# Expert tiles of the second layer in split precision, and second weights that stay resident in the third layer

## The reference

```
# L1: layernorm with gain and shift, 8 experts, top 2, capacity = ceil(2 * 1792 / 8) = 448 tokens each
hmid    = gelu(einsum('ecd,edf->ecf', exp_in, W1) + b1)     # 256 -> 1024
exp_out = einsum('ecf,efd->ecd', hmid, W2) + b2             # 1024 -> 256
x       = x + sum over the 2 chosen experts of exp_out * gate
# L2: layernorm, 8 experts, top 1, no capacity
h = relu(einsum('nd,edm->enm', x, W1) + b1)                 # 256 -> 1024
y = einsum('enm,emd->end', h, W2) + b2                      # 1024 -> 256
x = x + y[chosen expert] * probability
```

## Time and profile before

| | us |
|---|---|
| median of 3 runs | 3487.58 (3485.43 to 3488.54) |
| the profiled execution | 3493.5, of which the span of its instructions is 3491.7 |
| tile stage L0t | about 519.6 to 790.3 |
| tile stage L1t | about 1252.0 to 1483.4 |
| tile stage L2t | about 2266.2 to 2445.3 |

### The profile page before, as it was taken

The page is one execution under the profiler, slowest core; times in us unless marked ns, Lnnn a source line. Parts: engine busy times, 40 slices in busy tenths (PEclk is TensorE's granted clock), DMA queues, the critical chain, the costliest instruction groups (busy, mean ns, idle before and its releaser), DMA issues. The chain is left out here.

```text
span 3491.7 us, 60671 instructions
## 1 busy us (share of the span) xinstructions
PE 3171.1 (91%) x21982; PEld 2617.9 (75%) x21982; DVE 1555.4 (45%) x3343; ACT 1527.9 (44%) x4145; POOL 1308.9 (37%) x1417
## 2 busy tenths in 40 slices
PE   5888869998989869989999999699899999996999
PEld 4777758996666646668888887588788888875998
DVE  4777750004566520044444444300444444445766
ACT  2555524443355512245555555234455555552332
POOL 0000001113100011057777776310577777773343
PEclk8999959999999879999999999699999999997999
DMA  6556536542100234110000000298000000001433
GB/s 145 131 133 137 118 130 204 182 166 82 38 1 1 88 93 119 60 32 15 15 15 15 15 13 1 77 320 276 27 13 13 13 13 13 11 1 44 120 103 90
DMA packets 154741, 269.25 MB, mean 77 GB/s; under 512 B 50396, under 2 KB 129753, under 8 KB 140393
## 3 DMA queue, kind: packets, MB, share of 16 engines
q1 hardware_dynamic: 140840, 239.95, 23.2%
q0 software_dynamic: 8064, 20.20, 2.2%
q10 hardware_dynamic: 5568, 5.51, 0.5%
HBM read 231.13 MB, written 34.46 MB: 76 GB/s over the span
## 5 line engine op out<-in xcount | busy, mean ns | idle before, releaser
L718 POOL TENSOR_SCALAR L_probs<-L_probs,L_inverse 112x375 f32<-112x375 f32 x512 | 653.0, 1275 | 119.5 <-issue 119.5
L866 DVE TENSOR_REDUCE L_negmax<-bank 112x1 f32<-112x375 f32 x768 | 394.6, 542 | 431.7 <-PE bank L470 356.9
L674 ACT ACTIVATE L_probs<-bank,L_negmax 112x375 f32<-112x375 f32 x768 | 435.2, 572 | 219.6 <-DVE L_negmax L866 214.7
L497 PE MATMUL bank<-ident,L_probs 112*125 112x112 f32 x2304 | 399.6, 282 | 21.2 <-POOL L_probs L718 15.4
L497 PEld LDWEIGHTS bank<-ident,L_probs 112*125 112x125 f32 x2304 | 338.8, 190 | 92.6 <-issue 50.9
L716 POOL TENSOR_TENSOR L_inverse<-L_sums,neg_one 112x1 f32<-112x1 f32 x512 | 297.1, 580 | 142.2 <-ACT L_probs L674 141.8
L654 ACT ACTIVATE L_probsT<-bank 125x336 f32<-125x336 f32 x512 | 231.9, 453 | 248.1 <-PE bank L497 248.1
L636 ACT ACTIVATE v<-bank 125x512 f32<-125x512 f32 x192 | 114.8, 598 | 267.4 <-PE bank L423 267.4
L704 POOL TENSOR_TENSOR L_stats<-L_stats,neg_half 112x1 f32<-112x1 f32 x48 | 27.1, 564 | 517.7 <-DVE L_stats L783 517.7
L512 PE MATMUL bank<-L_probsT,v 125*64 125x112 f32 x3072 | 206.1, 269 | 2.4 <-ACT L_probsT L654 1.1
L416 PE MATMUL bank<-L_ctx_hi,L_wk_hi 128*128 128x376 f32 x512 | 149.3, 373 | 29.8 <-DVE L_ctx_lo L850 22.1
(11 more groups left out here) (305 smaller groups left out, 6968.0 us busy)
## 6 DMA issues: line engine op xcount, KB each, us to landing
L2t_w<-in_F_w SPq DMA_DIRECT2D x42, 1024.0 KB, 5.1
L0t_w<-in_F_w SPq DMA_DIRECT2D x35, 1024.0 KB, 5.0
L_keys<-spread_k SPq DMA_DIRECT2D x64, 376.0 KB, 6.4
L_ctxT<-in_ctxT SPq DMA_DIRECT2D x48, 375.0 KB, 3.3
tile_w<-in_F_w SPq DMA_DIRECT2D x16, 1024.0 KB, 5.8
L3d_row<-comb_rows SPq DMA_DIRECT2D x64, 224.0 KB, 3.3
w_all<-in_F_w SPq DMA_DIRECT2D x8, 1024.0 KB, 13.6
L_q<-spread_q SPq DMA_DIRECT2D x128, 56.0 KB, 2.2
```

The source lines that it names most:

```text
L497: ins = pe.transpose(psT[h % len(psT)][0:SJ, j * T:(j + 1) * T], probs[h % NB][:, j * SJ:(j + 1) * SJ], core.ident[0:T, 0:T])
L674: act.activation(probs[e % NB][:, :], psS[e % 2][0:T, 0:S], ACT.Exp, bias=negmax[b.par][:, e:e + 1], accum_out=sums[b.par][:, e:e + 1]).th ...
L718: pool.tensor_scalar(probs[h % NB][:, :], probs[h % NB][:, :], inverse[b.par][:, h:h + 1], None, ALU.mult)\
L866: dve.tensor_reduce(negmax[b.par][:, h:h + 1], psS[h % 2][0:T, 0:S], AX, ALU.max, negate=True).then_inc(maxed.sem, 1)
```

## The change

L1's tile stage is a new function, `capacity_tiles`. A tile is still one expert with 448 tokens. ScalarE rounds `w1`, `w2` to their hi halves (copies of 128x2048); VectorE makes their lo halves, both halves of the gathered rows and both halves of each hidden part of 128x448. TensorE runs three fp32r products for each float32 product before. The `w2` product is turned: the weights are now stationary and 448 tokens stream, so its output is transposed (`yT`); VectorE adds `b2`, TensorE transposes it back (8 transposes, `turn_out`), and ScalarE takes it out. The weights have one raw buffer each and are split a tile ahead; `b1`, `b2`, gain and shift of all experts are loaded in the routing stage.

L2's tile stage becomes `resident_tiles`, which L0 uses already: `w2` of all 8 experts is loaded in the routing stage, and the 4 MB for the cross attention of L3 move from the routing stage to tile 1 of the tile stage.

```diff
@@ -1499,6 +1499,8 @@
                 load(1)
                 for t in range(NT):
                     if t == 1:
+                        sp.wait_ge(all_weights.sem, all_weights.at(16 * E))
                         for dst, src, sem in next_loads:
                             sp.dma_start(dst, src).then_inc(sem, 16)
                     if t + 2 < NT:
...
+def capacity_tiles(nc, core, name, w, tile, NT, func):
+...
+                for e in range(NT):
+                    if e + 1 < NT:
+                        (w1_to, w1_from, w1_sem), (w2_to, w2_from, w2_sem) = cap_weights(core, w, e + 1)
+                        sp.wait_ge(w1_split.sem, w1_split.at(e + 1))
+                        sp.dma_start(w1_to, w1_from).then_inc(w1_sem, 16)
+                        sp.wait_ge(w2_split.sem, w2_split.at(e + 1))
+                        sp.dma_start(w2_to, w2_from).then_inc(w2_sem, 16)
+                    if e:
+                        store(e - 1)
+                store(NT - 1)
+...
+                def gather(e):
+                    if e >= 2:
+                        pool.wait_ge(xT_made.sem, xT_made.at(e - 1))
+                    for c in range(CH):
+                        pool.indirect_dma_start(
+                            out=xs[e % 2][:, c, :], out_offset=None, in_=core.tokens[:, :],
+                            in_offset=bass.IndirectOffsetOnAxis(ap=core.rows_of[0:CW, e * CH + c:e * CH + c + 1], axis=0))\
+                            .then_inc(rows_here[e % 2].sem, 16)
+...
+                def up(e, f):
+                    if f == 0:
+                        pe.wait_ge(w1_split.sem, w1_split.at(e + 1))
+                        pe.wait_ge(x_split.sem, x_split.at(e + 1))
+                    pe.wait_ge(h_taken.sem, h_taken.at(F * e + f - 1))
+                    for m, (wt, x) in enumerate(((w1_hi, x_hi), (w1_hi, x_lo), (w1_lo, x_hi))):
+                        for k in range(DC):
+                            ins = pe.matmul(psH[f % 2][:, 0:tile], wt[:, k, f * P:(f + 1) * P], x[:, k, :],
+                                            start=(m + k == 0), stop=(m + k == DC + 1))
+                    ins.then_inc(h_made.sem, 1)
+                def down(e, f):
+                    if f == 0:
+                        pe.wait_ge(w2_split.sem, w2_split.at(e + 1))
+                        pe.wait_ge(y_taken.sem, y_taken.at(e))
+                    pe.wait_ge(low.sem, low.at(F * e + f + 1))
+                    for half in range(DC):
+                        at = slice(half * P, (half + 1) * P)
+                        for m, (wt, h) in enumerate(((w2_hi[e % 2], h_hi), (w2_hi[e % 2], h_lo), (w2_lo[e % 2], h_hi))):
+                            ins = pe.matmul(psY[half][:, 0:tile], wt[:, f, at], h[:, f, :],
+                                            start=(f + m == 0), stop=(f == F - 1 and m == 2))
+                    if f == F - 1:
+                        ins.then_inc(y_made.sem, 1)
+                def turn_out(e):
+                    pe.wait_ge(y_taken.sem, y_taken.at(e + 1))
+                    for i in range(2):
+                        pe.wait_ge(y_out.sem, y_out.at(2 * e + i - 1))
+                        for c in range(2):
+                            at = (2 * i + c) * CW
+                            for half in range(DC):
+                                ins = pe.transpose(psO[i][0:CW, c * D + half * P:c * D + (half + 1) * P],
+                                                   yT[:, half, at:at + CW], core.ident[:, :])
+                        ins.then_inc(y_turned.sem, 1)
+                turn_in(0)
+                for e in range(NT):
+                    for f in range(F):
+                        up(e, f)
+                        if e and f == 2:
+                            turn_out(e - 1)
+                    if e + 1 < NT:
+                        turn_in(e + 1)
+                    for f in range(F):
+                        down(e, f)
+                turn_out(NT - 1)
+...
+                def high_w1(e):
+                    act.wait_ge(w1_here.sem, w1_here.at(16 * e + 16))
+                    act.wait_ge(h_made.sem, h_made.at(F * e))
+                    act.activation(w1_hi[:, :, :], w1[:, :, :], ACT.Copy).then_inc(w1_high.sem, 1)
+...
+                def hidden_part(e, f):
+                    n = F * e + f
+                    act.wait_ge(h_made.sem, h_made.at(n + 1))
+                    act.wait_ge(low.sem, low.at(n - 1))
+                    act.activation(hidden[n % 2][:, :], psH[f % 2][:, 0:tile], func, bias=b1[:, e, f:f + 1])\
+                        .then_inc(h_taken.sem, 1)
+                act.wait_ge(small.sem, small.at(64))
+                high_w1(0)
+                take_xT(0)
+                high_w2(0)
+                for e in range(NT):
+                    for f in range(F):
+                        hidden_part(e, f)
+                        if e and f == 4:
+                            take_out(e - 1)
+                    if e + 1 < NT:
+                        high_w1(e + 1)
+                        take_xT(e + 1)
+                        high_w2(e + 1)
+                take_out(NT - 1)
+...
+                def split_x(e):
+                    dve.wait_ge(xT_taken.sem, xT_taken.at(e + 1))
+                    dve.wait_ge(h_made.sem, h_made.at(F * e))
+                    dve.tensor_copy(x_hi[:, :, :], xT[:, :, :])
+                    dve.drain()
+                    dve.tensor_tensor(x_lo[:, :, :], xT[:, :, :], x_hi[:, :, :].bitcast(F32), ALU.subtract)\
+                        .then_inc(x_split.sem, 1)
+...
+                def split_hidden(e, f):
+                    n = F * e + f
+                    dve.wait_ge(h_taken.sem, h_taken.at(n + 1))
+                    if f == 0:
+                        dve.wait_ge(y_made.sem, y_made.at(e))
+                    dve.tensor_copy(h_hi[:, f, :], hidden[n % 2][:, :])
+                    dve.drain()
+                    dve.tensor_tensor(h_lo[:, f, :], hidden[n % 2][:, :], h_hi[:, f, :].bitcast(F32), ALU.subtract)\
+                        .then_inc(low.sem, 1)
+                def take_y(e):
+                    dve.wait_ge(y_made.sem, y_made.at(e + 1))
+                    dve.wait_ge(y_turned.sem, y_turned.at(2 * e))
+                    for half in range(DC):
+                        ins = dve.tensor_scalar(yT[:, half, :], psY[half][:, 0:tile], b2[:, e, half:half + 1], None, ALU.add)
+                    ins.then_inc(y_taken.sem, 1)
+                dve.wait_ge(small.sem, small.at(64))
+                split_w1(0)
+                split_x(0)
+                split_w2(0)
+                for e in range(NT):
+                    for f in range(F):
+                        split_hidden(e, f)
+                    if e + 1 < NT:
+                        split_w1(e + 1)
+                        split_x(e + 1)
+                        split_w2(e + 1)
+                    take_y(e)
...
     def tile_loads(w):
         out = []
-        for e in range(2):
-            for n in ("w1", "b1", "w2", "b2"):
-                src = w[n][e].partition_broadcast(T) if n == "b2" else w[n][e]
-                dst = h[f"tile_{n}_{e}"]
-                out.append((dst[everything[len(dst.shape)]], src, sem(f"w_here{e}")))
-        return out
+        for n in CAP_HELD[2:]:
+            out.append((h["cap_" + n][everything[len(h["cap_" + n].shape)]], w[n], sem("small_here")))
+        return cap_weights(core, w, 0) + out
...
-                    lambda: expert_tiles(nc, core, "L1t", f1, CAPACITY, TILES["L1"], ACT.Gelu, False))),
+                    lambda: capacity_tiles(nc, core, "L1t", f1, CAPACITY, TILES["L1"], ACT.Gelu))),
             lambda: cross_attention(nc, core, "L2", a["ctxT"], l2, 64, topk=2)),
         lambda: held(
             wide,
-            routing("L2", f2, 1, "all", TILE, lambda: wide_loads(l3)),
-            lambda: expert_tiles(nc, core, "L2t", f2, TILE, TILES["L2"], ACT.Relu, True),
+            lambda: held({"w2_all": [P, 8, 8, D]},
+                         routing("L2", f2, 1, "all", TILE, lambda: resident_loads(f2)),
+                         lambda: resident_tiles(nc, core, "L2t", f2, TILE, TILES["L2"], ACT.Relu, wide_loads(l3))),
```

111 lines of the change are left out of this document (106 added, 5 removed).

## The result

| | before | changed |
|---|---|---|
| median of 4 runs, us | 3488.06 (3485.43 to 3490.5) | 3450.32 (3441.31 to 3457.09) |
| ratio to before (95% interval) | | 0.9876 [0.9853, 0.9898] |
| span of the profiled execution, us | 3491.7 | 3448.0 |

The change makes the kernel 1.24% faster, 37.7 us by the medians. Forecast were 3443 and a difference of 44.7 us. The measured 3450.3 lies at the upper edge of the forecast's own range, 3436 to 3451.

What follows compares the result with a forecast made beforehand. TensorE was taken to bound L1t, with DMAs sharing the bound in L2t. L1t -37.7 and L2t -7.0 took 3487.6 to 3442.9, about 3443 us; own range 3436 to 3451, wider range with two rivals 3431 to 3462.

Steps and rivals of the forecast that it cites:

- Products of L1t: L1t, first to last product: 768 fp32r products at 0.204 us make 173.0 us instead of 215.2, a term of -42.2.
- Weight loads: Rival, L1t: weight loads not hidden, each product 0.375 us, kernel 3574 us; decides from 0.262 us a product; chance 0.04.
- VectorE's pace: L1t hidden parts: rival that VectorE needs 1.49 us a part and TensorE waits, +17, 3460 us; chance 0.17.
- TensorE stays ahead by little: L1t: a hidden part costs VectorE 1.1 us and TensorE makes one every 1.22, so TensorE sets the pace.
- the rival of 0.17: L1t: slow casts and stretched subtractions (0.85 us) let VectorE set the pace, 3460 us; chance 0.17.
- Splits for the next tile: L1t: VectorE's splits end 9.2 us after the last `w1` product, hidden under `w2` products, 3.7 us of `w2` products left.
- The end of L1t: L1t's end: the store now waits for additions, transposes, last copy and three hand-overs, +2.7 us.
- The start of L1t: L1t's start: ScalarE's first `w1` copy fits before the rows arrive; only the rows' halves stand on the path, +1.8 us.
- L2t's pace and start: L2t takes L0t's 7.24 us a tile, -8.8 us, and its earlier start, -1.2 us.
- The stall before tile 3: L2t: 4 MB for cross attention queue ahead of tile 3's weights, +3 us within bounds 0 and 6.
- worst case: L2t: tile 3's weights land at worst 29 us after the first product, against 24.8 when the tile is due.
- the third layer gives nothing: Rival, L2t: wide loads stall tile 3 by the upper bound, later weights queue, L2t keeps its time; 3450 us, chance 0.07.

Runs made afterwards that it cites:

- The two experiments: Changed kernel with each hidden part's cast done twice, then three times: 3453.96 us (0.9894 of before) and 3471.58 us (0.992).
- hold: Changed kernel, but VectorE waits in L1t's first tile for the four gathers before subtracting for w1's low half: 3450.1 us, 0.9889 of before.
- only_l2: Kernel before with only L2's tile stage changed, and SyncE's new wait in `resident_tiles`: 3497.36 us, 1.0003 of before.

## Why the prediction was right, point by point

- **Products of L1t.** Forecast from the first to the last 173.0 us, measured 1442.90 + 0.37 - 1273.33 = 169.9 (the last product is in the rows on the end of the stage below). The rate was 0.2025 and not 0.204, the transposes took 0.70 and 0.79 us instead of 0.77 and 0.9, and the first group lost less to the half clock (11.8 us against 12.7). What is left of a tile, 21.21 - 96 x 0.2025 - 0.70 - 0.79 = 0.28 us, has the size of the 0.25 put down for hand-overs, but the rows show no wait: it is slower products behind the transposes. Term -45.3 for -42.2. One sentence of the prediction was false: the trace of before does show fp32r products of 448 columns, in the dense stage, which I overlooked:

```profile
3303.84 0.37 PE L1972 MATMUL bank<-L3d_hid_hi,dense_w_hi 128*128 128x448 f32 x1
...
3304.88 0.37 PE L1972 MATMUL bank<-L3d_hid_hi,dense_w_lo 128*128 128x448 f32 x1
```

  Five products lie between those starts, 0.208 us each; the line through 376 and 512 columns was as good. By the formula for an isolated warm product in the Trainium skill, "TensorE: Matmul & The Clock Gate", section "Back-to-back issue gap", it would have been 0.189: the trace does not agree at 448 columns either, with 0.2025, and the difference is 10 us over the 768 products.
- **Weight loads** are hidden: at the full clock the products stand 0.20 to 0.21 us apart, but for the first one or two behind a set of transposes (up to 0.29). That is below the 0.262 from which this rival would have decided, and far from its 0.375.
- **VectorE's pace.** The forecast that TensorE stays ahead was right for a wrong reason. The step from 1.1 us of VectorE for a hidden part and 1.22 of TensorE to "TensorE stays ahead by little" compared rates within a phase, and the rival of 0.17 rested on it. The two experiments showed that a phase may run late and only the sum over a tile counts, with 5.5 us to spare. The rival's other leg, a stretched subtraction, didn't come either: beside gathers the subtractions kept their 0.626 and 2.29 us, and only gathers stretched. In the trace of before, the six long ones of rows 4 (1.16 to 1.28 us) all stand beside arithmetic of GpSimd (the longest, at 2849.66, beside an operation on `L_probs` from 2849.57 on) and none beside a gather. 17% was too much for it.
- **Splits for the next tile** are hidden, with the last done 8.9 us after the last `w1` product; forecast 9.2.
- **The end of L1t** was forecast at +2.7, and came so. From TensorE's last product on (timeline):

```profile
1442.90 0.37 PE L1942 MATMUL bank<-L1t_h_hi,L1t_w_lo 128*128 128x448 f32 x1
1443.30 1.28 DVE L2068 TENSOR_SCALAR L1t_yT<-bank,cap_b 128x448 f32<-128x448 f32 x2 [7.96 <-PE bank L1942]
```

  From the last product's end, 1443.27, to the next stage, at 1257.31 + 192.9 = 1450.2, it is 6.9 us. Before it was 1252.04 + 231.4 - 1479.19 = 4.2. That is +2.7.
- **The start of L1t** was mis-sized. The step in which ScalarE's first copy of `w1` fits ahead of the rows' arrival and only the halves of the rows then stand on the path (+1.8) took the rows' arrival as fixed. The first product came 16.0 us after the table load instead of 11.9: +4.1. 2.4 of it is the later arrival, which `hold` gave back; the other 1.7 are the halves, forecast at 1.8. I had weighed the stretching of gathers against VectorE's pace alone, where it costs nothing, and not where a gather is itself what all wait for. The Trainium skill, "SBUF — State Buffer", section "Who interferes with whom", says that an operation of VectorE with two inputs in SBUF and a GpSimd instruction that reads SBUF shut each other out. By that rule the trace agrees for a subtraction that comes first: the gather issued during it ended at 1263.71, so with its usual 0.92 us it began about where the subtraction ended, at 1262.91. For a gather that comes first it doesn't: the subtraction that began at 1287.79, within the gather of 1287.55, still took 2.29 us (at what point of its 0.93 us a gather reads SBUF, the trace doesn't show).
- **L2t's pace and start** were right: 7.24 us a tile, and the first product 10.25 us after the table load, which is 1.0 less than before (forecast 1.2).
- **The stall before tile 3** was the other mis-sized term: +3 within bounds of 0 and 6, measured 5.2 + 1.6 = 6.8, and 5.2 to 7.5 over eight traces. The prediction had the weights at worst 29 us after the first product; they came 2271.2 - 2241.65 = 29.6 after it, and 4.5 behind the last wide load (2254.14 + 12.5 = 2266.6). So its worst case was the true one, and I had leaned away from it because fewer other transfers share the DMAs. What I left out is that TensorE comes out of such a wait at the half clock. L2t gave 3.4 us between the first two traces instead of 7.0.

Sum of the terms as measured in the two first traces: -45.3 + 4.1 + 2.7 for L1t, -3.4 for L2t, in all -41.9, against the forecast of -44.7. The medians differ by 37.7, and the interval of the ratio reaches from 36 to 51 us.

The sum came that near partly by luck: the products gave 3.1 us more than forecast, and the start and the stall took 2.3 and 3.8 more. Nor does the whole time tell the forecast from its rival "the third layer gives nothing", which named 3450, the time that was measured. It is the stages that speak against that rival, with 3 to 8 us less in L2t; the whole time of `only_l2` doesn't.

## What to carry to other kernels

Replacing a float32 product by three fp32r products paid here at 448 columns (0.61 us for 0.75), with the halves made beside it; no other length was run. Whether VectorE can do that is a sum over a tile that its buffers span, not a rate within one phase. Look at where the first data of a stage are gathered: here a VectorE subtraction with two SBUF inputs, put beside the last gather, delayed the whole stage by 2.4 us. Put bulk loads for a later stage behind the next tile's load and one a tile, since the wait that they cause (5.2 us here) is followed by products at the half clock (1.6 us more). L0t still has such a gap.

## What the runs showed of the hardware that was not expected

- A gather on the GpSimd queue that meets a VectorE subtraction of 2.29 us takes 1.96 to 2.18 us instead of 0.93, and moving the subtraction moves which gather is long. The subtraction itself keeps its time, also when the gather began first (1287.55 against 1287.79). The rows' landing was 2.4 to 2.6 us later for a gather that was 1.0 longer.
- After 5.0 us without products the mean granted clock was 0.69 in the next 5.5 us, and 32 products took 5.31 us instead of 3.73.
- 5 MB in one DMA queue were served in order at 342 to 423 GB/s, and the last 1 MB was there 15.5 us after its issue.
- fp32r products of the same shape at the full clock came at 0.202 us in some executions and at 0.206 in others, for a stage of 280 us, and at both paces within each tile of L1t, the slower one behind the transposes back.
